# The edge-count matrix from one-hot products on TensorE instead of scatter-adds on GpSimd

## The reference

```python
def _gat_conv(x, src, dst, W, a_src, a_dst, bias, heads, out_ch, n_nodes):     # L0, twice
    h = (x @ W).reshape(n_nodes, heads, out_ch)
    e = leaky_relu(alpha_s[src] + alpha_d[dst], 0.2)
    m = segment_max(e, dst); ex = exp(e - m[dst]); denom = segment_sum(ex, dst)
    out = segment_sum(h[src] * (ex / denom[dst])[:, :, None], dst)
...
agg = segment_sum(norm[:, None] * (h[row] + edge_fea), col)    # L1, five layers: a sum over edges of h[src]
...
```

## Time and profile before

| | us |
|---|---|
| three timed runs | 4120.74, 4135.0, 4138.16 |
| median | 4135.0 |
| span of the profiled execution | 4111.2 |
| attention loop in it | 228.9 to 1703.7 |
| PE, PEld busy | 3273.1, 2215.9 |
| DVE, ACT, POOL busy | 2226.4, 1340.9, 2136.4 |

### The profile page before, as it was taken

How to read it: one execution, slowest core, us unless ns; L and a number is a source line. 1 busy time by engine, 2 the same in 40 slices (tenths; PEclk the granted TensorE clock), 3 DMA queues, 4 the chain that set the end, 5 groups by cost and what they waited for, 6 DMA issues and landing times. The chain is left out here.

```text
span 4111.2 us, 65888 instructions
## 1 busy us (share of the span) xinstructions
PE 3273.1 (80%) x17046; PEld 2215.9 (54%) x17047; DVE 2226.4 (54%) x7140; ACT 1340.9 (33%) x3098; POOL 2136.4 (52%) x1893
## 2 busy tenths in 40 slices
PE   0758888888887878769999999996976777777778
PEld 0446666666655555546555555554455555555544
DVE  5657777777777777772222222225244445554468
ACT  3123333333333333232213131314553333433322
POOL 4366777777788888544454636310004545554510
PEclk9878898888989898879999999997998888888889
DMA  7468656656665556334444545342943323332320
GB/s 302 64 172 261 140 142 145 141 141 145 138 140 133 139 135 138 64 83 133 156 144 141 172 126 170 124 130 52 263 119 93 91 85 96 94 94 87 90 55 21
DMA packets 472113, 530.37 MB, mean 129 GB/s; under 512 B 192361, under 2 KB 376791, under 8 KB 471925
## 3 DMA queue, kind: packets, MB, share of 16 engines
q0 software_dynamic: 142496, 237.86, 24.0%
q1 hardware_dynamic: 316808, 271.48, 22.5%
q10 hardware_dynamic: 12749, 20.33, 1.4%
HBM read 438.46 MB, written 70.54 MB: 124 GB/s over the span
## 5 line engine op out<-in xcount | busy, mean ns | idle before, releaser
L1136 PE MATMUL p_out<-rows,hot 128*128 128x266 f32 x2048 | 665.4, 454 | 68.2 <-DVE rows L1273 53.5
L2217 POOL DMA_INDIRECT col_rows<-col_dram,m_idx x440 | 417.6, 949 | 473.1 <-ACT m_idx L2297 333.3
L1061 POOL DMA_INDIRECT count_dram<-number,place x348 | 587.9, 1689 | 144.9 <-issue 107.7
L1053 POOL DMA_INDIRECT rows<-att_dram,idx x512 | 526.1, 1028 | 216.7 <-issue 143.0
L1705 POOL DMA_INDIRECT rec_dram<-records,edge_place x416 | 407.8, 980 | 429.6 <-PE p_hi L1738 200.6
L1634 PE MATMUL p_lo<-cbuf,parts 128*128 128x400 f16 x1750 | 583.4, 333 | 5.1 <-issue 5.1
L1635 PE MATMUL p_hi<-cbuf,parts 128*128 128x400 f16 x1750 | 583.4, 333 | 4.0 <-issue 4.0
L1136 PEld LDWEIGHTS p_out<-rows,hot 128*128 128x128 f32 x2048 | 409.8, 222 | 170.1 <-DVE rows L1273 85.2
L1144 PE MATMUL p_out<-mask,ident_bf 128*128 128x240 bf16 x1788 | 361.4, 287 | 1.7 <-issue 1.7
L1273 DVE TENSOR_TENSOR rows<-rows 128x512 f32<-128x512 f32 x512 | 349.8, 684 | 0.2 <-issue 0.2
L1662 DVE TENSOR_TENSOR node_sum<-p_hi,low_sb 128x400 f32<-128x400 f32 x80 | 46.0, 574 | 557.5 <-ACT low_sb L1653 491.6
(11 more groups left out here) (421 smaller groups left out, 6126.7 us busy)
## 6 DMA issues: line engine op xcount, KB each, us to landing
cbuf<-count_dram SPq DMA_DIRECT2D x40, 2500.0 KB
dl_rep<-dl_dram SPq DMA_DIRECT2D x128, 256.0 KB
count_dram<-zeros SPq DMA_DIRECT2D x20, 1000.0 KB
g_rows<-count_dram SPq DMA_DIRECT2D x25, 800.0 KB, 4.7
rec_dram<-blank ACTq DMA_DIRECT2D x1, 17600.0 KB
m_group_rows<-rec_dram SPq DMA_DIRECT2D x110, 160.0 KB
records<-in_edges POOLq DMA_DIRECT2D x32, 520.0 KB
key_rep<-key_dram SPq DMA_DIRECT2D x64, 256.0 KB
```

The source lines that it names most:

```text
L1053: nc.gpsimd.indirect_dma_start(rows[r][:, u, :], None, att_dram, bass.IndirectOffsetOnAxis(ap=idx[r][:, u:u + 1].bitcast(U32), axis=0)).th ...
L1061: nc.gpsimd.indirect_dma_start(count_dram, bass.IndirectOffsetOnAxis(ap=place[r][:, n, c:c + 1].bitcast(U32), axis=0), number[r][:, 2 * n ...
L1136: m = nc.tensor.matmul(p_out[q][:, side, 0:HALF], hot[k][:, u, :], rows[k][:, u, side * HALF:(side + 1) * HALF], start=(u == 0), stop=(u = ...
L2217: nc.gpsimd.indirect_dma_start(col_rows[q][:, u, :], None, col_dram, bass.IndirectOffsetOnAxis(ap=idx[q][:, u:u + 1].bitcast(U32), axis=0) ...
```

## The change

The keys are no longer scattered. The 3200 destinations are taken in windows of ten (`WD`); of a window's part of the count matrix, 128 source rows modulo 128 by 25 source tiles times 10 destinations are held as 128 x 250 numbers. Six **key steps** (`CS`) of 128 keys belong to each group, so 768 in all. For a key step POOL makes a one-hot by source modulo 128 (`lo_hot`, 128 x 128) behind its gathers, DVE makes a one-hot by source tile and destination (`key_hot`, 128 x 250), and PE multiplies the two into `counts`, six blocks of PSUM. ACT copies the six blocks (128 x 1500, strided) into the memory of `x_sb`, as float16 (`taken`, the same bytes), and once a round SP writes four groups' windows, 240 columns, to `count_dram`. A window that continues from the last group is brought back by `carry`. Where each key step's product, the copy and the store go is read into registers from small tables. Since `x_sb` is used in this way, it is saved to `x_dram` at the loop's start and loaded again behind it.

With this the zero fill, `alike`, `if_first`, `at_place`, `key_rep`, all scatters and `keep_clock` go. `p_out` becomes one buffer instead of two, `p_in` with `p_run` and `p_top` with `p_tab` share a bank. The plan block loses the key comparisons of 32 chunks and gets some 16 small DVE instructions, 8 of 104 x 768, 28 products and 6 copies that sort the keys into key steps. POOL computes the tables in the weights block (19 instructions on one partition).

```diff
                     def _(sp):
-                            sp.dma_start(key_rep[q][:, 0:n, :].rearrange("p u e -> p (u e)"),
-                                         key_dram[bass.ds(i * (BODY * P) + (PRE + first) * P, n * P)].partition_broadcast(P)).then_inc(rep_in[q], 16)
+                            if isinstance(g, int) and g == 1:
+                                sp.dma_start(x_dram, x_sb[:]).then_inc(x_out, 16)
+                            if k == 3 and not is_first(i):
+                                store(i - 1, i)
+                        def store(r, i):
+                            sp.wait_ge(evacuated, i * 4)
+                            sp.nop().then_inc(waits_passed, 1)
+                            sp.wait_ge(stored, i * 16)
+                            sp.nop().then_inc(waits_passed, 1)
+                            table = store_table[:].rearrange("o r v -> o (r v)")
+                            (to,) = read_registers(nc, table, r * 2, 1, ET.SP, PITCH - WIDE)
+                            (side,) = read_registers(nc, table, r * 2 + 1, 1, ET.SP, AT)
+                            sp.dma_start(count_dram.rearrange("(k p) n -> p k n", p=P)[:, :, bass.ds(to, WIDE)],
+                                         taken[:, :, bass.ds(side, WIDE)]).then_inc(stored, 16)
...
                     def _(act):
+                        def evacuate(b, n, r):
+                            act.wait_ge(counted, n)
...
+                            if r is not None and not is_first(r):
+                                act.wait_ge(stored, r * 16)
+                            (at,) = read_registers(nc, take_table[:].rearrange("o r k -> o (r k)"), b, 1, ET.Activation, HALVES - CS * WD)
+                            nc.scalar.copy(taken[:, :, bass.ds(at, CS * WD)].rearrange("p k (v d) -> p v k d", v=CS),
+                                           counts[:].rearrange("p (v c) -> p v c", v=CS)[:, :, 0:WC].rearrange("p v (k d) -> p v k d", d=WD)
+                                           ).then_inc(evacuated, 1)
                         def work(j, k, i):
                             act.wait_ge(arg_ready, j + 1)
                             nc.scalar.activation(slots(k), zz[:], ACT.Exp).then_inc(weight_ready, 1)
+                            if not is_first(j):
+                                evacuate(j - 1, j, i if k == 1 else None)
...
                     def _(pool):
-                            if k % 2 == 0:
-                                pair(k, 0, before)
...
+                                for u in range(U):
+                                    gather((k + 3) % 4, u)
+                            if within(j, 1):
+                                pool.wait_ge(low_ready, j + 1)
+                                if not is_first(j):
+                                    pool.wait_ge(counted, j)
+                                low_hots(j + 1, (k + 1) % 2)
+                        def low_hots(b, q):
+                            nc.gpsimd.tensor_copy(lo_now[:], lo_step[:, bass.ds(b * CS, CS)]).then_inc(low_there, 1)
+                            pool.wait_ge(low_there, b + 1)
+                            pool.nop().then_inc(waits_passed, 1)
+                            for v in range(CS):
+                                m = nc.gpsimd.tensor_scalar(lo_hot[q][:, v, :], iota_bf[:], lo_now[:, v:v + 1], None, ALU.is_equal)
+                            m.then_inc(low_ready, 1)
...
                     def _(pe):
+                        def clear(j):
+                            pe.wait_ge(empty_ready, 1 if is_first(j) else 2)
+                            if not is_first(j):
+                                pe.wait_ge(evacuated, j)
+                            for v in range(CS * AT // HALVES):
+                                nc.tensor.matmul(counts[:, v * HALVES:(v + 1) * HALVES], ident16[:], nothing[:], start=True, stop=False,
...
                     def _(dve):
+                        def count_hots(g, q, first, last):
+                            for v in range(first, last):
+                                one = TS(key_hot[q][:, v, :], iota_key[:], column(key_step, g * CS + v), None, ALU.is_equal)
```

More of the change, by code:

```diff
@@ L1158, in work @@
+                            for v in range(CS // 2):
+                                count(q, v, at[v])
+                            add_up(j, k, 2)
+                            for v in range(CS // 2, CS):
+                                m = count(q, v, at[v])
+                            m.then_inc(counted, 1)
                             if within(j, 2):
```

467 lines of the change are left out of this document (222 added, 245 removed).

## The result

The changed kernel is **slower**: 4264.2 us median (4258.7 to 4281.2, 4 runs) against 4133.9 (4120.7 to 4138.2, 4 runs), a ratio of 1.033 with a 95% interval of 1.030 to 1.036. The forecast was 4067, in a range of 3960 to 4190.

The account below looks back on a forecast made before the run. The prediction took a ring between DVE and PE to bound the loop: 128 groups falling from 11.35 to 11.0 us give -45, blocks outside -23, so 4135 - 68 = 4067 us, in a range of 3960 to 4190.

Parts of the forecast that it names:

- The bound of before: Attention loop before the change: no engine full in early groups, POOL nearly full only late; mean 11.35 us a group.
- the ring of DVE and PE: Attention loop: DVE and PE wait on each other each group, so removing POOL work gains little unless this shortens.
- the 0.8 from which they would bind: POOL's seven small instructions a group: taken at 0.3 us each, POOL would bind from 0.8 us each.
- The ring at full clock: Chain of DVE and PE work from one zz to the next after the change, PE at full speed: 10.4 us.
- The clock: PE at its lower level 10 to 20% of the time after the change, giving 11.0 us a group.
- as long as now: Rival, chance 0.17: period stays 11.3 to 11.6 us, only blocks outside the loop gain; 4106 to 4144 us.
- The rival on the slow side: PE's register loads delay the first add_up, period from 11.7 us; chance 0.20, of which 0.05 for POOL binding.
- DVE, ACT: Loop work after the change: DVE 8.3 to 9.8 us a group, under the period; ACT's copy hidden before clear.
- late groups like early ones: Sign of being right: zz 11.0 us apart in late groups of the loop as in early ones.
- a clock under 0.85: Sign of being wrong: PE's granted share of full speed below 0.85, where before it was 0.87 and 0.90.
- The wait for the turned scores: Sign of being right: DVE's wait for p_in in the loop, 42.6 us before, gone.
- Outside the loop: Blocks around the attention loop: plan block -22, ahead of the loop -9, behind it +8, together -23 us.

Follow-up runs that it names:

- e11: Changed kernel without POOL's one-hots from the second group on (counts wrong); 4253 us, 1.030 of the kernel before.
- e3: Changed kernel with twelve filler products of 240 columns ahead of PE's register loads; 3886 us, 1.015 of the kernel before.
- e8: Changed kernel with clear, carry, count products and both register loads moved behind the next group's turn_back; 4061 us, 0.985 of the kernel before.
- e2: Changed kernel with constants instead of PE's two register loads a group (counts in wrong blocks); 3843 us, 1.003 of the kernel before.
- e10: Changed kernel with short register loads: four values from a table of their own, two read singly; 4170 us, 1.012 of the kernel before.
- e17: Changed kernel with short register loads and twelve fillers ahead of the loads; 3862 us, 1.010 of the kernel before.
- e6: Changed kernel with loads moved behind turn_back and ten fillers spread over three places; 4104 us, 0.997 of the kernel before.
- e5: Changed kernel unaltered, run again on the first kind of chip; 4261 us, 1.033 of the kernel before.
- e7: Kernel before with two register loads a group behind node_tops, four values read from place 4i; 4121 us, 0.999 of the kernel before.
- e12: Changed kernel with count products behind the next group's turn_back, short loads and ACT's copy later; 4098 us, 0.994 of the kernel before.
- e9: Kernel before with two register loads a group behind node_tops, four values read from place 4i + 1; 4152 us, 1.009 of the kernel before.
- e16: Changed kernel unaltered, on the second kind of chip; 3965 us, 1.037 of the kernel before.

## Why the prediction was wrong

**The bound of before: right in kind.** That POOL's scatters were not what bound the early groups, and that taking them off bought little unless the ring of DVE and PE got shorter, held: POOL idles 3.6 us a group after, and e11 shows that even its one-hots are free. They took 0.62 each, twice what I took, still under the 0.8 from which they would bind. The shared port of the Trainium skill, "SBUF - State Buffer", section "Who interferes with whom", played no part that these runs show: without POOL's one-hots DVE's are as long as with them, 282 and 283 ns (e11).

**The ring at full clock: right, as far as it goes.** I bounded the two loads by 0.7 and 2.0, had the first `add_up` start at 3.2 to 4.5, and took 0.4 for them. They take 1.53, and the first `add_up` starts at 4.39 on average. At the upper level it would end at 5.44, and that is the start of the second that the forecast had, 5.0 + 0.4. With `clear` to the third `add_up` at 1.08, as in the group at 671, and DVE's second `weigh` ending at 4.8 where I had 5.0, the terms of the full clock hold.

**The clock: the step that failed.** "Ten products of real work come in their place", with a low share of 10 to 20% spread over all work, worth 0.6 us a group (11.0 over 10.4). The products come later in the group, not where PE idles, and don't hold the clock up ahead of the first `add_up`. So PE is at its lower level in the same place of every group, in work that is in the chain. Means of 108 groups from 300 to 1650, counted from `zz`:

| | forecast at full clock | measured |
|---|---|---|
| second `add_up` ends, `clear` starts | 6.45 | 7.97 |
| third `add_up` starts | 7.5 | 9.68 |
| `look_up` starts | 9.1 | 11.06 |
| next `zz` | 10.4 | 12.45 |

The two `add_up` bring 1.5 us over the forecast, `clear`, `carry` and the first count products another 0.7, and behind them nothing is added. Together that is 2.1, where 0.6 was taken for the clock. The share of time at the lower level is 46% (0.77) instead of the 26% of before. Fillers ahead of the `add_up` bring 0.65 a group (e3), and the products themselves put there bring 1.45 (e8, with the loads gone from the ring too). The rival "as long as now" supposed before's share, and even it fell short.

**What the loads cost by this.** 0.4 was right only at full clock, where the second `add_up` waits for `weigh` until 5.0 anyway. With the first one at 1.9 us nothing hides them: without loads the period falls by 0.98 (e2), with short ones by 0.58 (e10). So the same wrong clock made the price of the loads wrong. I had the row that warned of their length, 1.0 us for four values in the loop, and set it beside 0.59 for eight without asking why fewer cost more. The place decides: 0.33 from 4i, 1.0 from 4i + 1. The Trainium skill, "Runtime: NRT & Kernel Launch", section "Instruction fetch mechanics", gives some 200 ns a register, for loads that it describes as coming from HBM. Five would be 1.0 us by it (an estimate), near the 1.23 measured here from a table in SBUF, and the 0.33 of four at a multiple of four does not agree.

Loads and clock overlap, and the split between them depends on which is taken first: 0.58 and 0.65 alone, 0.83 together (e17), 1.13 with the loads moved and the fillers spread over three places (e6).

**The rival on the slow side: right mechanism, half of the cause.** It named the register loads and a period from 11.7 on. It was given 0.15, too little, since its price stood in a row: at 12.3 it had 4234 us, with 12.44 and 4264 measured. It named the loads alone, and with the long loads and fillers the period is 11.58 (e3), so it takes the low clock as well to get to 12.4.

**DVE, ACT.** One-hots 0.31 for 0.3, the copy 1.42 for 1.55, DVE busy 448 of 700 and never full; right. Of the signs that the prediction gave, late groups like early ones and POOL's 3.6 us of waiting came true, and so did a sign of being wrong, a clock under 0.85. The wait for the turned scores was to go and became DVE's largest instead, 200.6 us in 700.

**Outside the loop** I had -23, and the profile shows -8.0, -10.0, +11.2, -4.2, together -11.0. The plan block gave 8 instead of 22. I put the stretched `in_tile` on the zeros. They are stretched without zeros too:

```profile
48.24 0.65 DVE L633 SCALAR_TENSOR_TENSOR in_tile<-src_tile,iota_row,every 128x416 bf16<-128x416 f32 x1 [0.64 <-issue]
75.28 0.43 DVE L643 TENSOR_SCALAR hi_row<-src_raw 104x512 int32<-104x512 int32 x1 [6.45 <-remote]
```

The stretch goes with POOL's gathers of the node rows, which run from 39.9 to 73.4, and DVE then waits 6.45 us, until just behind the last of them; that is argued from the times only, no run took the gathers away. The projection without the late scatters, costed at nothing, is 4.2 us shorter. The 17 us that L1 to L3 took more are not shown to be the change's: the stretch from the last `node_sum` to the last `u_agg` takes 1294.9 in the profile of before, 1310.5 in that of the change, 1303.8 in e5, and 1307.5 in e7, which is before's own program there. The 17 us are thus within what one program shows from run to run, and they are most of the 20 us by which the spans differ more than the medians.

**What stays open.** What made e12 slower than e8. Why the kernel before has a longer period on one kind of chip than on the other, while the version outside the ring has not, so that it gains 1.5% on one and 0.2 to 0.4% on the other. Why the clock falls about `node_tops`: the runs only show that it falls where PE had idled (0.78 us in the changed kernel, 0.81 in e2, 2.04 in e3) and ran seventeen-column products, and that it stayed up in e8, where the idle time ahead of them was 0.16.

## What to carry to other kernels

Put new work of an engine where that engine waits, not into the chain that others wait for: the same products and their loads cost 200 us less behind `turn_back` than among the `add_up`. A register load is a serial piece of the stream, and its price must be taken from the row with the same number and the same place in the table; when two rows of one kind of instruction disagree, find out why before a value between them is taken. A lower clock costs only where the engine carries the ring, so its share of time says nothing until it is known in which instructions it falls. And a wait that hides a piece of work at full clock may hide nothing at the lower one, so a term that was taken as hidden has to be worked out at both.

## What the runs showed of the hardware

Register loads of PE take 0.30 us for one value, 0.33 for four from a multiple of four, 1.00 for four from one place behind it, 1.23 for five from 6j + 1, and 0.59 for eight from 8i + 4. The longer load of four, behind `node_tops` in the kernel before, lowered the granted clock between 300 and 1000 from 0.88 to 0.80, and between 1080 and 1650 from 0.87 to 0.86 (e7, e9). GpSimd's `tensor_scalar` of 128 x 128 bfloat16 takes 0.62 us. The gathers take 1.13 us after and 1.03 before, and the one-hots are not the reason, since they take 1.12 without them (e11). In the changed kernel PE falls to its lower level in every group, behind 0.8 us of idling and 1.07 us of seventeen-column products, and comes back by the end of the two `add_up` that follow in some groups, and only during or behind `clear` in more than half. Two kinds of chips gave 4125 and 3827 us for one kernel. For the changed kernel the difference is 296 us (e5, e16), and 234 of them lie between the last `node_sum` and the last `u_agg` (1303.8 and 1069.6).
